# Attention's opening: six PSUM banks for the pairs of tiles, and weights split as they land

## The reference

```python
x = x + 0.5 * ffn(layernorm(x))       # 8 experts, capacity 1024, top-1 by router
x = x + attention(layernorm(x))
x = x + 0.5 * ffn(layernorm(x))
# attention: 16 heads of 16 dims, T = 1024, batch 8
q, k, v = heads(x @ Wq.T + bq), heads(x @ Wk.T + bk), heads(x @ Wv.T + bv)
q, k = rope(q), rope(k)               # pairs of neighbouring dims turned by an angle
att = softmax(where(causal, q @ k.T / 4, -1e10))
x_att = (att @ v) @ Wp.T + bp
```

## Time and profile before

| | |
|---|---|
| median of 3 runs | 2623.69 us (2612.97 to 2627.59) |
| the profiled execution | 2642.3 us |
| its span, first to last instruction | 2640.5 us |
| mean granted TensorE clock | 0.922 |
| opening of attention, first load to first maximum | 572.6 to 719.7 us |
| one pair in the opening | 20.7 us |

### The profile page before, as it was taken

How to read it: one execution, slowest core, us unless ns; L and a number is a source line. 1 busy time by engine, 2 the same in 40 slices (tenths; PEclk the granted TensorE clock), 3 DMA queues, 4 the chain that set the end, 5 groups by cost and what they waited for, 6 DMA issues and landing times. The chain is left out here.

```text
span 2640.5 us, 43228 instructions
## 1 busy us (share of the span) xinstructions
PE 2226.4 (84%) x14740; PEld 1457.2 (55%) x14740; DVE 1690.9 (64%) x5140; ACT 1249.4 (47%) x2506; POOL 942.5 (36%) x1344
## 2 busy tenths in 40 slices
PE   5739999945599999999999999998994773899997
PEld 5729999943334444443444444443332673799997
DVE  7326556533378778788887877887772662465563
ACT  1224444421046656666666665666673432344443
POOL 3534344316523333333333333332000465244442
PEclk9999999975579999999999999999997875999999
DMA  9372322221624453544534435335324423422220
GB/s 347 147 245 69 109 80 72 72 75 40 155 57 100 102 118 81 122 101 99 118 90 114 109 80 114 98 89 118 83 55 125 161 93 126 167 73 97 92 73 22
DMA packets 187148, 283.22 MB, mean 107 GB/s; under 512 B 14616, under 2 KB 149976, under 8 KB 178736
## 3 DMA queue, kind: packets, MB, share of 16 engines
q1 hardware_dynamic: 172592, 247.08, 34.2%
q0 software_dynamic: 14336, 33.38, 3.6%
HBM read 153.99 MB, written 126.88 MB: 106 GB/s over the span
## 5 line engine op out<-in xcount | busy, mean ns | idle before, releaser
L1683 ACT ACTIVATE at_probs<-at_score_ps 128x512 f32<-128x512 f32 (+3 forms) x1536 | 692.5, 497 | 451.3 <-PE at_score_ps L1800 312.0
L1559 DVE CUSTOM_DVE_ANT_0 at_junk<-at_max_ps,at_causal 128x128 f32<-128x128 f32 (+3 forms) x1024 | 485.3, 484 | 124.8 <-PE at_max_ps L1786 123.2
L1786 PE MATMUL at_max_ps<-at_k,at_q 96*128 96x512 bf16 (+3 forms) x1536 | 493.1, 339 | 44.1 <-DVE at_peak L1559 32.0
L1797 PE MATMUL at_score_ps<-at_q,at_k 99*128 99x512 bf16 (+3 forms) x1536 | 498.0, 331 | 9.2 <-DMA at_v<-v_rows 4.2
L1562 DVE TENSOR_REDUCE at_peak<-at_max_ps 128x1 f32<-128x512 f32 x512 | 351.9, 687 | 114.4 <-PE at_max_ps L1786 111.5
L1786 PEld LDWEIGHTS at_max_ps<-at_k,at_q 96*128 96x128 bf16 x1536 | 144.3, 98 | 398.7 <-DVE at_peak L1559 193.6
L1056 DVE TENSOR_TENSOR f_hid_lo<-f_hid,f_hid_hi 128x512 fp32r<-128x512 f32 x256 | 177.4, 693 | 285.2 <-ACT f_hid_hi L1080 274.6
L1810 PE MATMUL at_o_ps<-at_probs,at_v 128*32 128x512 f32 (+3 forms) x3072 | 336.8, 511 | 1.2 <-ACT at_probs L1683 0.7
L1077 ACT ACTIVATE f_hid<-f_hid_ps 128x512 f32<-128x512 f32 x256 | 153.1, 598 | 377.4 <-PE f_hid_ps L1103 374.1
L1118 PE MATMUL f_y_ps<-f_w_hi,f_hid_hi 128*128 128x256 f32 x1024 | 290.7, 284 | 18.5 <-DVE f_hid_lo L1056 18.5
L1118 PE MATMUL f_y_ps<-f_w_hi,f_hid_lo 128*128 128x256 f32 x1024 | 291.1, 284 | 0.0
(11 more groups left out here) (178 smaller groups left out, 3647.8 us busy)
## 6 DMA issues: line engine op xcount, KB each, us to landing
f_w_raw<-in_w SPq DMA_DIRECT2D x32, 1024.0 KB, 7.7
qk<-at_parts SPq DMA_DIRECT2D x32, 768.0 KB, 4.2
expert_in<-r_zeros SPq DMA_DIRECT2D x16, 1040.0 KB, 15.9
f_xe<-expert_in SPq DMA_DIRECT2D x32, 520.0 KB, 4.0
v_rows<-at_v_outs SPq DMA_DIRECT2D x32, 512.0 KB, 6.2
at_v<-v_rows SPq DMA_DIRECT2D x32, 512.0 KB, 10.6
o_rows<-at_o_out SPq DMA_DIRECT2D x64, 256.0 KB, 2.0
at_q<-qk SPq DMA_DIRECT2D x32, 384.0 KB, 7.7
```

Of the source, the lines that this page charges most:

```text
L1559: v.tensor_tensor_reduce(junk[bank(k, r)][:, 0:w], src, causal[:, HALF - w:HALF], 1.0, LEAST, ALU.add, ALU.max, out).then_inc(max_used, 1)
L1683: a.activation(probs[t % 2][:, h, c0:c0 + w], score_ps[(GH * t + h) % BANKS][:, 0:w], ACT.Exp, scale=float(SCALE)).then_inc(exp_done, 1)
L1786: te.matmul(max_ps[bank(u, r)][:, 0:w], q[u][0:ROWS, h, i * P:(i + 1) * P], kk[u][0:ROWS, h, k0:k0 + w], start=True, stop=True).then_inc(m ...
L1797: last = te.matmul(out[:, 0:w], kk[u][:, h, j * P:(j + 1) * P], q[u][:, h, hf * HALF + c0:hf * HALF + c0 + w], start=True, stop=not diagonal)
```

## The change

Three things are changed in the opening. First, the weights get their own semaphore (`w_loaded`) and are split as soon as they have landed, while biases and constants (`c_loaded`, now 8 loads) are waited for later; the order of VectorE's first instructions changes with it. The `v_outs` fill goes to GpSimd, and the fill of each `kk` goes to the end of VectorE's turns 0, 1 and 2.

Second, pairs 0 to 5 use six banks: one for the turned x (`EARLY_XT`), two for q and k (`EARLY_QK`), one for v (`EARLY_V`), two for the rotated rows (`EARLY_ROT`). TensorE's order in turn n is: turn x of pair n, all products of pair n (`early_products`), then the rotated rows of pair n - 1 (`early_turns`). VectorE and ScalarE follow that order; `add_bias_v(n - 1)` comes after `xt_low(n)`. Pair 4's rotated rows are split in turn 5, and pair 5's v bias is added after the first maxima.

Third, the third parts of these pairs go from GpSimd to VectorE, GpSimd's last stage of `rope` waits until the rows rotated before are turned, and the output bias (`add_output_bias`) of pairs 0 to 5 goes to the last six groups.

```diff
+        w_loaded = sem("w_loaded")
...
+        w_lo_ready = sem("w_lo_ready")
...
+        EARLY_XT, EARLY_QK, EARLY_V, EARLY_ROT = max_ps[0], max_ps[1:3], score_ps[0], score_ps[1:3]
+
         def peaks_in_ps(k, r):
...
-            sp.dma_start(w_raw[:, :, 0:C], dr["wq_t"].rearrange("(c p) o -> p c o", p=P)).then_inc(c_loaded, 16)
-            sp.dma_start(w_raw[:, :, C:2 * C], dr["wk_t"].rearrange("(c p) o -> p c o", p=P)).then_inc(c_loaded, 16)
-            sp.dma_start(w_raw[:, :, 2 * C:3 * C], dr["wv_t"].rearrange("(c p) o -> p c o", p=P)).then_inc(c_loaded, 16)
+            sp.dma_start(w_raw[:, :, 0:C], dr["wq_t"].rearrange("(c p) o -> p c o", p=P)).then_inc(w_loaded, 16)
+            sp.dma_start(w_raw[:, :, C:2 * C], dr["wk_t"].rearrange("(c p) o -> p c o", p=P)).then_inc(w_loaded, 16)
+            sp.dma_start(w_raw[:, :, 2 * C:3 * C], dr["wv_t"].rearrange("(c p) o -> p c o", p=P)).then_inc(w_loaded, 16)
             for n, b in enumerate((dr["bq"], dr["bk"], dr["bv"])):
...
                     last.then_inc(rope_step, 1)
                 if stage == 2:
...
+                    if n >= 1:
+                        pool.wait_ge(rt_ps_ready, 2 * (n - 1) + s + 1)
...
             def third_parts(n, s):
...
+            for s in range(2):
+                p.memset(v_out[s][:, :, :, D:VW], 1.0).then_inc(ones_ready, 1)
+                pool.wait_ge(ones_ready, s + 1)
             invert_std(0)
-            pool.wait_ge(c_loaded, 16 * 11)
+            pool.wait_ge(c_loaded, 16 * 8)
             for n in range(LEAD - 1):
                 invert_std(n + 1)
                 for s in range(2):
                     for stage in range(3):
...
-                add_output_bias(n)
-                for s in range(2):
-                    third_parts(n, s)
             invert_std(LEAD)
             for stage in range(3):
...
-            add_output_bias(LEAD - 1)
             move_peaks(0, 0, 0)
             move_peaks(0, 0, 1)
...
                         if t in (3, 5):
...
-                    if prepare and t == 4:
-                        add_output_bias(n)
+                    if t == 4:
+                        add_output_bias(n % PAIRS)
                     if t == 6 and more:
                         move_peaks(g + 1, slot_round(g, k, 1)[0], 0)
                     if prepare:
...
                 last.then_inc(xn_ready, 1)
...
-            def xt_low(n):
+            def xt_low(n, bank=prep_ps):
...
-                v.tensor_tensor(xt_lo[:].rearrange("p s c t -> p (s c t)"), prep_ps[:],
+                v.tensor_tensor(xt_lo[:].rearrange("p s c t -> p (s c t)"), bank[:],
...
-            def add_bias_qk(n, s):
+            def add_bias_qk(n, s, bank=prep_ps):
...
-                v.tensor_tensor(qk[s][:], prep_ps[:], bias[:, 0:2 * C], ALU.add).then_inc(qk_ready, 1)
-
-            def add_bias_v(n):
+                v.tensor_tensor(qk[s][:], bank[:], bias[:, 0:2 * C], ALU.add).then_inc(qk_ready, 1)
+
+            def add_bias_v(n, bank=prep_ps):
...
                 for s in range(2):
...
-                                           prep_ps[:, s * C:(s + 1) * C].rearrange("p (g h d) -> p g h d", d=D, h=GH),
+                                           bank[:, s * C:(s + 1) * C].rearrange("p (g h d) -> p g h d", d=D, h=GH),
...
                 last.then_inc(v_ready, 1)
...
-            def leave(n, s):
+            def leave(n, s, bank=prep_ps):
...
-                v.tensor_tensor(rest[s][:], prep_ps[:].rearrange("p (c t) -> p c t", t=P),
+                v.tensor_tensor(rest[s][:], bank[:].rearrange("p (c t) -> p c t", t=P),
...
+
+            def third_parts(n, s):
+                dve.wait_ge(part1_ready, 2 * n + s + 1)
+                v.tensor_tensor(part[2][:, :, s * P:(s + 1) * P], rest[s][:], part[1][:, :, s * P:(s + 1) * P],
+                                ALU.subtract).then_inc(part2_ready, 1)
...
             def ring(g, k, r):
...
-            for k in range(SLOTS):
-                v.memset(kk[k][ROWS:ROWS_M], 1.0)
-            for s in range(2):
-                v.memset(v_out[s][:, :, :, D:VW], 1.0)
-            dve.wait_ge(c_loaded, 16 * 11)
+            measure(0)
+            dve.wait_ge(w_hi_ready, 1)
+            v.tensor_tensor(w_lo[:], w_raw, w_hi[:].bitcast(F32), ALU.subtract).then_inc(w_lo_ready, 1)
+            normalize(0)
+            dve.wait_ge(c_loaded, 16 * 8)
...
-            dve.wait_ge(w_hi_ready, 1)
-            v.tensor_tensor(w_lo[:], w_raw, w_hi[:].bitcast(F32), ALU.subtract).then_inc(ones_ready, 1)
-            measure(0)
-
-            def head(n):
-                normalize(n)
+            dve.wait_ge(ones_ready, 2)
+            for n in range(LEAD):
...
-                xt_low(n)
-                add_bias_qk(n, 0)
-                add_bias_v(n)
-                add_bias_qk(n, 1)
-
-            for n in range(LEAD - 1):
-                head(n)
+                xt_low(n, EARLY_XT)
+                if n >= 1:
+                    add_bias_v(n - 1, EARLY_V)
                 for s in range(2):
-                    leave(n, s)
-            head(LEAD - 1)
+                    add_bias_qk(n, s, EARLY_QK[s])
+                if n + 1 < LEAD:
+                    normalize(n + 1)
+                if n >= 1:
+                    for s in range(2):
+                        leave(n - 1, s, EARLY_ROT[s])
+                    for s in range(2):
+                        third_parts(n - 1, s)
+                if n < SLOTS:
+                    v.memset(kk[n][ROWS:ROWS_M], 1.0).then_inc(ones_ready, 1)
...
                 if RING[r] == SECOND:
...
+            add_bias_v(LEAD - 1, EARLY_V)
...
         def _(act):
...
-            def xt_high(n):
+            def xt_high(n, bank=prep_ps):
...
-                a.copy(xt_hi[:].rearrange("p s c t -> p (s c t)"), prep_ps[:]).then_inc(xt_hi_ready, 1)
-
-            def first_parts(n, s):
+                a.copy(xt_hi[:].rearrange("p s c t -> p (s c t)"), bank[:]).then_inc(xt_hi_ready, 1)
+
+            def first_parts(n, s, bank=prep_ps):
...
-                a.copy(part[0][:, :, s * P:(s + 1) * P], prep_ps[:].rearrange("p (c t) -> p c t", t=P)
+                a.copy(part[0][:, :, s * P:(s + 1) * P], bank[:].rearrange("p (c t) -> p c t", t=P)
...
             def second_parts(n, s):
...
-            act.wait_ge(c_loaded, 16 * 11)
+            act.wait_ge(w_loaded, 16 * 3)
...
-            for n in range(LEAD - 1):
-                xt_high(n)
-                for s in range(2):
-                    first_parts(n, s)
-                    second_parts(n, s)
-            xt_high(LEAD - 1)
+            for n in range(LEAD):
+                xt_high(n, EARLY_XT)
+                if n >= 1:
+                    for s in range(2):
+                        first_parts(n - 1, s, EARLY_ROT[s])
+                    for s in range(2):
+                        second_parts(n - 1, s)
...
             def body(g, k, more, prepare, finish):
...
         def _(pe):
...
-            def transpose_x(n):
+            def transpose_x(n, bank=prep_ps):
...
                 for s in range(2):
...
-                        last = te.transpose(prep_ps[:, c0:c0 + P], xn[s][:, cc * P:(cc + 1) * P], sh.ident[:])
+                        last = te.transpose(bank[:, c0:c0 + P], xn[s][:, cc * P:(cc + 1) * P], sh.ident[:])
                 last.then_inc(xt_ps_ready, 1)
...
                 if s == 1:
                     last.then_inc(v_ps_ready, 1)
...
-            def transpose_qk(n, s, half):
+            def transpose_qk(n, s, half, bank=prep_ps):
                 if half == 0:
...
                     if s == 0:
...
-                    last = te.transpose(prep_ps[:, c * P:(c + 1) * P], rot[s][:, c * P:(c + 1) * P], sh.ident[:])
+                    last = te.transpose(bank[:, c * P:(c + 1) * P], rot[s][:, c * P:(c + 1) * P], sh.ident[:])
                 if half == 1:
                     last.then_inc(rt_ps_ready, 1)
...
                 last.then_inc(pv_done, 1)
...
-            pe.wait_ge(ones_ready, 1)
-
-            def head(n):
-                pe.wait_ge(rest_ready, 2 * n)
-                transpose_x(n)
-                for i in range(3):
-                    product_qk(n, 0, i)
+            def early_products(n):
+
+                pe.wait_ge(xt_lo_ready, n + 1)
                 for s in range(2):
-                    product_v(n, s)
-                for i in range(3):
-                    product_qk(n, 1, i)
-
-            for n in range(LEAD - 1):
-                head(n)
+                    pe.wait_ge(qk_ready, max(2 * (n - 1) + s + 1, 0))
+                    for i in range(3):
+                        last = product(EARLY_QK[s][:], s, 0, 2 * C, i)
+                    last.then_inc(qk_ps_ready, 1)
+                    if s == 0:
+                        pe.wait_ge(v_ready, n)
+                        for k in range(2):
+                            for i in range(3):
+                                last = product(EARLY_V[:, k * C:(k + 1) * C], k, 2 * C, C, i)
```

(27 more changed lines are left out.)

## The result

The changed kernel takes **2606.2 us** (median of 5 runs, 2604.0 to 2613.1) against 2622.9 for the kernel before (5 runs), a ratio of 0.9945 with a 95% interval of 0.9925 to 0.9964. An identical copy, timed later beside seventeen more runs of before, gave 2602.0 against 2623.9, a ratio of 0.9918 (0.9903 to 0.9933). Two runs of before among all that were timed beside the changed versions were slow (3493.8 and 4727.1 us), and the ratios leave them out. So the change makes the kernel faster by 0.5 to 0.8%, some 14 to 22 us. I had forecast a gain of 35 us and a range up to 2607: the first median lies in it by less than 1 us, but the gain is about half of what I had forecast.

What follows compares the result with a forecast made beforehand. A chain round the engines through one PSUM bank, plus pair 5's store wait, bounds the opening: pairs 5.5 and pair 5 20.4 give 25.9, clock 9.3, gain 35.2; 2623.7 - 35.2 = 2588.5, say 2589 us; range 2574 to 2607.

Steps and rivals of the forecast that it cites:

- Head, loads, the end of the opening: Before pair 0, x's low part comes 9.3 us sooner; at the end, maxima start 13.5 us after group 0's first load.
- the store's wait: v's bias waits for the store of two pairs ahead, 5.9 us after third parts; turn 4's v products 1.5 late.
- 20.4 of my sum: End of the opening: 20.4 us gained because pair 5 no longer stands between the loads and the maxima.
- The clock: TensorE's clock rises to 1.00, 4.4 us (or 5.5) into each turn's unbroken products; worth 9.3 us in all.
- Rival (a): Opening: small gaps between groups of products keep the clock at 0.50; gain 25.9 us, chance 0.15.
- Fills: kk memsets at the end of VectorE's turns 0, 1 and 2: 4.3 us each, 12.9 us onto the path.
- What speaks against it: Third parts on VectorE beside GpSimd's rotations: at most 0.2 us each, 1.6 in four turns, left out of the sum.
- the forecast opening: From the first load of x to the first maximum: 684.5 - 572.6 = 111.9 us.
- the forecast with the clock: Opening's pair chain with the clock's rise: third parts 2.25 us earlier in each of turns 1 to 3; maxima at 684.5.
- Rival (b): Opening: each VectorE third part waits for one whole GpSimd instruction, 8 x 1.16 = 9.3 us less; gain 25.9, chance 0.06.
- Rival (c): Opening's pair chain stays no shorter than 20.7 us for an unseen wait; maxima at 699.8, gain 19.9, chance 0.08.
- GpSimd's new wait for the turned rotations: In the pair chain, GpSimd's wait for the turned rotation of the pair ahead ends before it matters.

Runs made afterwards that it cites:

- warm: Changed kernel with 24 idle TensorE turns of the identity ahead of the products in turns 1 to 3; 2602.4 us, ratio to before 0.9938.
- norm_fills: norm_early plus kk fills off the turns: two on GpSimd before the first roots, one on VectorE before x lands; 2583.7 us, ratio to before 0.9864.
- norm_early: Changed kernel with VectorE's normalize(n+1) moved ahead of pair n's second qk bias; 2588.9 us, ratio to before 0.9863.
- fills_pool: Changed kernel with the three kk fills moved from VectorE's turns to GpSimd; 2596.4 us, ratio to before 0.9901.
- rot_late: Changed kernel with GpSimd's rotations in pairs 1 to 5 held until VectorE's third parts of the pair ahead are done; 2592.6 us, ratio to before 0.9886.
- best: norm_fills plus rot_late's held-back GpSimd rotations, against the changed kernel; 2582.9 us, ratio to before 0.9856.

## Why the prediction was wrong, step by step

- **Head, loads, the end of the opening: right.** First low part after 15.9 us (15.8 forecast), maxima 13.1 us behind group 0's first load (13.5), loads and not pair 5 the last to end. Only 2.8 us of the 23.6 come from group 0's loads starting sooner (110.4 against 113.2); the other 20.8 from pair 5 and the store's wait leaving the place between loads and maxima. That step, 20.4 of my sum, held. So did the store's wait: v's bias in turn 4 comes 5.9 us after the third parts, as forecast.
- **The clock: the mechanism right, its spread too narrow.** It rose 2.8 to 6.0 us into the products in the first profile and 3.2 to 9.2 in the copy, where I had taken 4.4 and, as the other end, 5.5. Rival (a), that it stays down, is out. In "warm" a high clock from the start was worth about 3 us in turn 1.
- **Fills: the size right, 4.4 us each on VectorE (4.3 forecast).** What they cost the opening is less than three of them, since the store's wait stands behind them in turns 2 and 3: taking all three off the turns gave 3.9 us (norm_fills against norm_early), and 7.3 in fills_pool (against 123.7), where normalize(0) lost 3.3 of it again.
- **What failed is the step "What speaks against it".** I had weighed GpSimd beside VectorE by the longest of 256 subtractions in another stage and set it at 0.2 us for each third part, left out of the sum. The longest of them is 0.88 us, where this opening has 1.77. The terms in its place: the third parts 0.9 to 1.1 a turn, and *normalize*, which I had not put on the list at all, 1.9 a turn (0.8 to 0.9 in turn 0). Four turns of 2.8 and 0.8 are 12.0; the forecast opening was 11.6 too short, and rot_late, which takes the four turns' share away, came in at 110.8 against 111.9.
- That the sum fits so well is partly luck. Against the forecast with the clock, the third parts of pairs 0 to 3 are late by 4.5, 7.9, 11.1 and 11.9 us in the first profile: turns 2 and 3 lost 3.3 each and turn 4 only 0.8, with the clock up early there. In the copy they are late by 3.6, 6.3, 9.2 and 12.2, which is near 0.8 for turn 0 and 2.8 for each later one, though turn 4 has a late clock in it.
- **The trace of before had the rows that I needed.** The longest VectorE row shows only one side of a meeting. In the stage of the earlier trace rows GpSimd's own instruction is the one held up: where a subtraction begins 0.08 us after it (506.15), the subtraction takes 0.71 and GpSimd's instruction 1.72 instead of 1.21, and others reach 1.96. And in the loop over the groups normalize itself meets GpSimd's addition, 25 times: the tile beside it takes 0.66 to 0.78 us, where all others take 0.40 to 0.41, and is done 0.15 us after the addition. All three rows are of the kernel before:

```profile
L979 POOL TENSOR_SCALAR f_xn<-f_xe x120: 1210/1243/1960, 168.7 to 2576.1; 128x256 f32<-128x256 f32 x120
...
795.36 1.28 POOL L1410 TENSOR_TENSOR at_rot<-at_by_cos,at_by_sin 128x512 f32<-128x512 f32 x1
...
796.01 1.10 DVE L1505 TENSOR_SCALAR at_xn<-x_sb,at_moments,at_rstd 128x256 f32<-128x256 f32 x2
```

- **Rival (b)** had the right mechanism (VectorE waits for one whole GpSimd instruction) and a price of 9.3, but named the third parts for it and had 0.06. **Rival (c)**, pairs no shorter than 20.7, gave what happened in turns 2 and 3 of the first profile to 0.1 us (of the copy to 0.7), for a wait "that I don't see". The gain that it gave, 19.9, is nearest to the two measured in the medians, 16.7 and 21.8; the opening's 23.6 lies between it and (b)'s 25.9. The wait of (b) was the one that (c) didn't see, so the two were one case and deserved more than their 0.14 together.
- GpSimd's new wait for the turned rotations, which I had costed at nothing, times the meeting: it lets GpSimd go on at 598.75, just as normalize begins at 598.81. No run leaves that wait out. Without it the addition could have ended before normalize, but GpSimd's next multiplication waits for the bias that ends at 598.89, so by these rows it would still have met normalize.

## What to carry to other kernels

When an instruction of VectorE is to run beside GpSimd, lay both timelines over each other and look at every VectorE instruction there that works from SBUF to SBUF, the unmoved ones too. Its price here was what remained of GpSimd's instruction, and of the next. Take the rows of that very instruction beside that engine, and look at both engines' rows: where one looks undisturbed, the other may have waited. A wait on GpSimd that puts its work into VectorE's idle time can be worth more than the added concurrency, here 9 to 13 us of the opening for one line. And a rule that speaks against a change is to be given the size that rule and rows of this instruction give, not the size of another instruction's longest row from another stage.

## What the runs showed of the hardware

Two VectorE instructions of 128x256, SBUF to SBUF, take 0.73 us alone, 1.51 beside one GpSimd instruction of 1.2 (norm_early), 2.59 beside two, 4.04 beside a GpSimd fill of 3.51 that reads nothing (fills_pool). Subtractions of two SBUF inputs take 0.69 alone and up to 1.77 beside GpSimd. `leave` and the bias additions, with PSUM as one input, keep their 0.69 beside GpSimd. VectorE's own fill keeps its 3.47 us beside GpSimd's two fills (best). The effect goes both ways: GpSimd's root step of 0.2 us took 1.67 beside VectorE's low part of the weights (1.76). The recorded starts don't tell who wins when they are close: in before a subtraction that starts 0.08 us behind GpSimd's instruction is let through (506.23), and in the changed kernel a normalize that starts 0.07 us ahead of GpSimd's multiplication (600.08) has to wait.
